# First attention of a fused two-attention, two-expert-layer kernel: the square roots of the first half sample taken unit by unit, without VectorE's product

## The reference, cut to what matters

```python
# for each of 16 heads, with q, k, v of 8 features and |q|^2, |k|^2 the squared norms
diff_sq  = max(|q|^2 + |k|^2 - 2 q.k, 0)
denom    = max((1 - |q|^2) * (1 - |k|^2), 1e-6)
cosh_arg = max(1 + 2 * diff_sq / denom, 1)
distance = arccosh(cosh_arg)          # 0 where cosh_arg is 1
attn     = softmax(-distance)         # over the 256 keys
out      = attn @ v, heads joined, @ Wo.T
```

## Time and profile before

| | |
|---|---|
| median of 3 runs | 1136.32 us |
| lowest, highest | 1131.87, 1139.19 us |
| span of the profiled execution, first to last instruction | 1128.1 us |
| its time by the list of runs | not given apart; the median stands 8.2 us above the span, the lowest 3.8 us |
| busy in the span: PE, DVE, ACT, POOL | 974.6, 982.1, 695.7, 354.8 us |
| mean granted TensorE clock | 0.859 of full |

### The profile page before, as it was taken

One profiled execution on the slowest core, in us unless ns is written; L12 is line 12 of the kernel. 1 busy time (PEld: TensorE's weight loads), 2 busy tenths in 40 slices (PEclk: granted clock), 3 DMA queues, 4 the chain that ended last, 5 costly groups with the idle time before them and its releaser, 6 DMA issues. The chain is left out here.

```text
span 1128.1 us, 17423 instructions
## 1 busy us (share of the span) xinstructions
PE 974.6 (86%) x5403; PEld 708.3 (63%) x5403; DVE 982.1 (87%) x1491; ACT 695.7 (62%) x794; POOL 354.8 (31%) x214
## 2 busy tenths in 40 slices
PE   7746676766768999999999899999759999999997
PEld 5523343434446888888888645444647888888886
DVE  7798889888978999999999797996598999999997
ACT  4759999999975455544444562667444544444554
POOL 2036555655550334333332120100012333333430
PEclk9865555555558999999999998999969999999999
DMA  2000000000104855555551000000028655555531
GB/s 57 1 1 1 1 0 1 1 1 1 36 15 97 217 153 147 153 148 158 151 155 40 1 1 1 1 2 1 1 71 196 168 149 157 151 156 153 150 90 37
DMA packets 36478, 85.16 MB, mean 75 GB/s; under 512 B 5968, under 2 KB 19280, under 8 KB 36432
## 3 DMA queue, kind: packets, MB, share of 16 engines
q1 hardware_dynamic: 36432, 84.56, 28.2%
HBM read 82.45 MB, written 2.10 MB: 75 GB/s over the span
## 5 line engine op out<-in xcount | busy, mean ns | idle before, releaser
L1324 ACT ACTIVATE sg<-ps 128x512 f32<-128x512 f32 x264 | 156.8, 594 | 265.6 <-PE ps L473 264.1
L473 PE MATMUL ps<-xh,whi 128*128 128x512 f32 x528 | 206.6, 391 | 1.3 <-ACT b L1189 1.3
L473 PE MATMUL ps<-xh,wlo 128*128 128x512 f32 x528 | 206.3, 391 | 0.0
L473 PE MATMUL ps<-xl,whi 128*128 128x512 f32 x528 | 206.2, 391 | 0.0
L2070 DVE TENSOR_TENSOR hf<-sg,ps 128x512 f32<-128x512 f32 x264 | 170.3, 684 | 32.0 <-DVE hl L2077 24.4
L1471 POOL TENSOR_TENSOR rr<-xr,rr 128x2048 f32<-128x2048 f32 x32 | 144.9, 4548 | 163.5 <-ACT xr L1170 149.4
L1518 POOL CAST whi<-wraw 128x384 fp32r<-128x384 f32 x66 | 66.4, 1006 | 369.7 <-PE ps L473 321.5
L2077 DVE TENSOR_TENSOR hl<-hf,hh 128x1024 fp32r<-128x1024 f32 x132 | 179.1, 1357 | 0.5 <-DVE hf L2070 0.5
L2082 DVE TENSOR_TENSOR hf<-hf,cbc 128x1024 f32<-128x1024 f32 x128 | 157.5, 1231 | 13.3
L1372 ACT ACTIVATE hh<-hf 128x1024 fp32r<-128x1024 f32 x132 | 139.2, 1054 | 4.8 <-DVE hf L2082 4.8
L1520 POOL TENSOR_TENSOR wlo<-wraw,whi 128x384 fp32r<-128x384 f32 x66 | 117.4, 1778 | 5.3
(11 more groups left out here) (259 smaller groups left out, 1581.1 us busy)
## 6 DMA issues: line engine op xcount, KB each, us to landing
cbc<-routing_coefficients SPq DMA_DIRECT2D x256, 256.0 KB, 3.8
wraw<-in_wexp_dram SPq DMA_DIRECT2D x66, 192.0 KB, 2.8
X<-in_x_dram SPq DMA_DIRECT2D x4, 256.0 KB, 4.9
routing_coefficients<-cT SPq DMA_DIRECT2D x8, 128.0 KB, 2.3
out_dram<-X SPq DMA_DIRECT2D x4, 256.0 KB, 2.9
rope_in<-in_consts_dram SPq DMA_DIRECT2D x1, 512.0 KB, 3.5
wa<-in_wA_dram SPq DMA_DIRECT2D x1, 256.0 KB, 4.2
w_in<-in_wB_dram SPq DMA_DIRECT2D x1, 128.0 KB, 3.3
```

The lines of the kernel that those rows point to most:

```text
L473: return pe.matmul(o, l, r, start=start, stop=stop, **kw)
L1324: act.activation(sg[c % 2][:, :], bank(4 + 2 * (c % 2)), ACT.Silu).then_inc(s_sg, 1)
```

## The change

The roots of half 0 (chunks 0 and 1, units 0 to 3) are taken unit by unit, on 128 x 1024 tiles, each as soon as its `ratio` is there. Both chunks get the two roots of the first form, so that chunk 1 needs no product, and its `logs` use the first form too. `product(1)` is not called, `s_P` counts one less, and ACT's wait on it is lowered by one. `s_R` is raised once for each chunk, as before. All other halves keep their form and order. The table load that opened half 1 is still there, and the number of table loads is the same.

```diff
-                for half in range(2 * B):
+                for U in range(4):
+                    at = slice(U % 2 * UC, (U % 2 + 1) * UC)
+                    act.wait_ge(s_X, U + 1)
+                    act.activation(rr[:, U // 2, at], xr[:, U // 2, at], ACT.Sqrt, bias=one_c[:, 0:1])
+                    last = act.activation(xr[:, U // 2, at], xr[:, U // 2, at], ACT.Sqrt)
+                    if U % 2 == 1:
+                        last.then_inc(s_R, 1)
+                act.preload_act_table_set("natural_log_exp_and_others")
+                logs(0, 1.0, None, -2.0)
+                for half in range(1, 2 * B):
                     even, odd = 2 * half, 2 * half + 1
...
-                    act.wait_ge(s_P, half + 1)
+                    act.wait_ge(s_P, half)
                     act.activation(o, o, ACT.Sqrt).then_inc(s_R, 1)
...
-                    if half >= 1:
+                    if half == 1:
+                        logs(1, 1.0, None, -2.0)
+                    else:
                         logs(odd - 2, 2.0, one_c[:, 0:1], -1.0)
                     logs(even, 1.0, None, -2.0)
...
                         ratio(U)
-                        if u % 4 == 3:
+                        if u % 4 == 3 and U > 3:
                             product(U // 2)
```

## The result

The changed kernel takes 1130.06 us, median of 21 runs (1124.68 to 1133.99), against 1133.32 us of the kernel before in as many (1129.12 to 1139.19). The ratio is 0.997, 95% interval 0.9958 to 0.9982: 2.0 to 4.8 us faster, within 1%. The first attention gave what was forecast, 5.8 us; between half and two thirds of it arrives in the time (3.3 us by the medians, 3.9 by the means). The profiled execution of the changed kernel took 1133.85 us at a span of 1132.1, so it is one of the longest of its 21, and its span must not be held against the 1128.1 of before. In every execution for which both are listed, the time lies 1.7 to 1.9 us above the span; so the 1128.1 us of before belong to an execution of about 1129.9 us (an estimate), one of the shorter ones of that kernel. The stage has to be compared by itself.

What follows compares the result with a forecast made beforehand. ACT was taken to bound the first attention, with one 6.8 us hole at its start. Gains of 5.59 + 0.06 + 0.1 = 5.75 us took 1136.32 to 1130.6 us; 8 in 10 range 1126.5 to 1136.5.

Steps and rivals of the forecast that it cites:

- The hole and its cause: Start of first attention: ACT waits 6.8 us once for DVE's product, which waits for POOL's first sum.
- mean of 3.19 us: Mean length of the 14 later products on DVE, between 2.29 and 5.76 us because of waiting for POOL's sums.
- The sum for half 0: ACT's last root of half 0 ends at 71.35 instead of 76.94, 5.59 us earlier (5.41 to 5.78).
- Half 1 and the bias: Half 1's root no longer waits for its product, 0.06 us; `logs(1)` without bias saves 0.1 us.
- The cover of the product: Half 1: DVE's product ends 0.17 us before ACT can begin its root.
- The slower rival: Half 1: DVE 2.7 us or more late, POOL's sum gets ahead of the product; 1.1 us slower, 1137.5; chance 0.04.
- From the stage to the time: Whole kernel: the 5.75 us gain passes on in full, span 1128.1 to 1122.3, median 1136.32 to 1130.6 us.
- The clock rival: Second attention: TensorE's low-clock time changes, costing at most half; less gain 0.14, more 0.13, slower than 1137 us 0.03.
- Something with its own clock: End of first attention: something else sets the stage's end, so the gain is not passed on; 1136.3 us, chance 0.06.
- The signs of being wrong: ACT wait of a microsecond or more before half 2; new ACT idle later; later stages' fast parts differing over two us.
- The number: Whole kernel: 1130.6 us, the median 1136.32 less 5.75 us.

Runs made afterwards that it cites:

- units only: Kernel before with only chunk 0's roots taken unit by unit, chunk 1 keeping product and single root: stage 265.29 us against 267.07.
- sum after product: Kernel before with POOL's first sum made to wait for DVE's first product: stage 264.98 us against 267.07.
- three delays: Changed kernel with three unused copies on DVE ahead of half 1's product: stage 268.14 us against 261.30.
- products for chunks 8, 16 and 24: Changed kernel with DVE's product and one root also for these even chunks: stage 258.69 us against 261.30, one execution 1122.15 us.
- six traces: Three traces each of the kernel before and the changed kernel, unmodified: stages 267.04 to 267.09 us and 261.27 to 261.30 us.
- two later comparisons: Changed kernel run again, unmodified, against the kernel before: ratios 0.9966 and 0.9979.

## Why the prediction was right, and where it was not

**The hole and its cause: right.** The product was late because POOL's sum held it. Four kernels moved the sum or the product (units only, sum after product, three delays, products for chunks 8, 16 and 24), and each time the product ended 2.15 us after the sum, or took 2.29 us where none was running. The prediction's reading of the mean of 3.19 us holds as well: 12 of those 14 products were held by a sum.

**The sum for half 0: right.** 5.59 us forecast, 17.67 - 12.06 = 5.61 measured. The pairs are of 1.15 and 1.04 us with 0.10 overlap, 2.09 in place of 2.05; that the last pair started 0.03 us after its `ratio` and not 0.09 made up for it, which is luck of a few hundredths.

**Half 1 and the bias: right.** The root comes at 82.59, 22.25 us after the first clamp, against 27.92: 5.67 us, forecast 5.59 + 0.06 = 5.65. The cover of the product is 0.15 us, forecast 0.17. The stage is 5.77 us shorter, forecast 5.75. ACT got no other idle time.

**The slower rival: not there, and rightly priced.** It appeared only with three copies on DVE.

**From the stage to the time: mis-sized.** The step that failed is "the span goes from 1128.1 to 1122.3 ... so I take the sum from the median". It took the later stages as moved and otherwise unchanged. The router's part did move as a whole, its end 33.5 to 33.6 us after the last logs in all six traces. Behind it, the changed kernel's traces spend more time at the lower clock level, at the first router, at the end of layer 1, in the second attention, behind the second router and at the end, and each of these costs 1 to 2.7 us. In time, 3.3 us by the medians of the 21 runs came through, 3.9 by their means. In the two later comparisons the means differ by 4.0 us (12 and 16 runs) and by 1.9 us (8 and 49 runs, on another chip than the 4.0). Weighted by their errors the three give 3.3 us, with a standard error of 0.5, so about 2.5 us of the 5.8 were given back.

**The clock rival: right in its price, not in its place.** It had 0.14 for less gain, at most half of the time spent more at the lower level. The traces show about half. But it was put on the low stretch of the second attention near 675 us, which every trace has; a further 3.4 us shortly ahead of it, in two of the three traces of the changed kernel and in one of before, is all that the second attention adds. "Something with its own clock" had 0.06 and was thought of as all or nothing.

**The signs of being wrong.** None of the three was met: ACT has no wait of a microsecond between its first root and half 2, it has no new idle time later in the stage, and the later stages differ by more than two us only through stretches of lower clock; where no such stretch lies, the parts agree to 0.4 us, the long loops of the layers to 1.9.

**The number.** 1130.6 us stood against 1130.06. Part of that is luck: the median of three runs of before, 1136.32, lay 3.0 us above that of 21, which about made up for the gain that was lost. All other runs bear out the sign and that it is within 1%.

## What to carry to other kernels

A product on one engine that spares another a function call is worth what each engine has left at that place: at the start of a pipeline, where the bound engine is still idle, give it the longer form, in the full stretch give it the shorter one. Where VectorE takes two inputs from SBUF and GpSimd works on SBUF beside it, as here, read an overlong instruction's end against the other engine's end before believing that it is slow, and count which of the two will start first after an edit. A gain well ahead of places where the granted clock changes should be credited in full only to its own stage. Compare stage lengths from several traces, and before saying where the rest went, check that the traced executions are as long as the others: here they put the loss at 6.8 us, where the times of all runs put it at 2.5.

## What the runs showed that was not expected

Three traces of a kernel can agree and still not stand for its executions. The tail of the last layer was 8.4 us in 3 of 3 traces of one kernel and 10.0 in 3 of 3 of another with the same code there, once at a granted clock of 1.00 and once with 3.4 us at 0.50; yet 10 of the second kernel's first 21 executions were shorter than its shortest trace. And an exclusive port takes its toll twice: a product put between two sums waits 1.6 us for the first and delays the second by 2.0 (11.10 against 9.06 us for the pair).
